# One GpSimd operation of 1024 columns fills the scan inputs of a block pair, with new engine orders and banks

## The reference

```python
xz = xn @ in_proj_w                      # 512 inner channels, then the gate z
x_c = silu(conv4(x_ssm) + conv_b)
x_dbc = x_c @ x_proj_w                   # dt (16), B (16 states), C (16 states)
dt = softplus(x_dbc[..., :R] @ dt_w + dt_b)
def step(h, inp):                        # over the 512 tokens
    xt, dtt, Bt, Ct = inp
    h = exp(dtt[..., None] * A) * h + (xt * dtt)[..., None] * Bt[:, None, :]
    return h, einsum('bn,bdn->bd', Ct, h)
y = (y + x_c * D_param) * silu(z)
x = x + alpha * attn_out + (1 - alpha) * (y @ ssm_out_w)
```

## Time and profile before

| | |
|---|---|
| median of three runs | 6051.18 us (6045.14 to 6052.57) |
| the profiled execution's own time | 6049.22 us |
| its span in the trace | 6047.2 us |
| busy share PE, DVE, POOL, ACT | 88%, 85%, 72%, 68% |
| granted TensorE clock, mean over the span | 0.959 |

### The profile page before, as it was taken

One profiled execution on the slowest core, in us unless ns is written; L12 is line 12 of the kernel. 1 busy time (PEld: TensorE's weight loads), 2 busy tenths in 40 slices (PEclk: granted clock), 3 DMA queues, 4 the chain that ended last, 5 costly groups with the idle time before them and its releaser, 6 DMA issues.

```text
span 6047.2 us, 117094 instructions
## 1 busy us (share of the span) xinstructions
PE 5294.5 (88%) x32280; PEld 3519.6 (58%) x32280; DVE 5128.6 (85%) x7776; ACT 4113.5 (68%) x6407; POOL 4329.0 (72%) x3569
## 2 busy tenths in 40 slices
...
GB/s 130 122 142 140 139 141 145 128 131 142 133 149 143 127 135 137 140 150 135 131 136 138 142 150 130 129 139 137 149 143 122 142 131 140 146 140 135 136 126 38
DMA packets 521729, 814.77 MB, mean 135 GB/s; under 512 B 80432, under 2 KB 227288, under 8 KB 520976
## 3 DMA queue, kind: packets, MB, share of 16 engines
...
q10 hardware_dynamic: 7904, 0.39, 0.1%
...
## 4 chain that ended last, share of the span: by engine, by line
PE 58%; DVE 15%; issue 11%; ACT 8%; POOL 4%; DMA 2%; ACTq 1%; SPq 1%; DVEq 0%; POOLq 0%
PE pY L939 8%; PE pM L1090 8%; PE pM L1081 6%; DVE mx L1258 4%; DVE pD L1200 4%; PE pM L1070 4%; PE pM L1014 3%; PE pM L948 3%; PE pM L961 3%; PE pM L981 3%; PE pM L1027 3%; PE pM L996 3%; PE pM L1045 2%; DMA region<-mrow 2%; ACT pD L707 2%
## 5 line engine op out<-in xcount | busy, mean ns | idle before, releaser
L584 POOL TENSOR_TENSOR state<-scan_in,bc 128x512 f32<-128x512 f32 x2048 | 2555.1, 1273 | 586.1 <-DMA bc<-bc_d 311.2
L1200 DVE TENSOR_TENSOR_SCAN pD<-pD,state 128x512 f32<-128x512 f32 x1536 | 1857.8, 1219 | 137.3 <-POOL state L584 81.0
L707 ACT ACTIVATE pD<-scan_in,A 128x512 f32<-128x512 f32 x2048 | 1403.7, 690 | 546.3 <-DVE state L1208 453.3
L939 PE MATMUL pY<-ident,state 128*128 128x128 f32 x8192 | 1209.3, 284 | 9.7 <-DVE state L1208 5.3
L939 PEld LDWEIGHTS pY<-ident,state 128*128 128x128 f32 x8192 | 944.1, 147 | 305.5 <-issue 187.4
L1208 DVE TENSOR_TENSOR state<-pD,bc 128x512 f32<-128x512 f32 x1536 | 1033.6, 682 | 27.3
L1258 DVE TENSOR_REDUCE mx<-pM 128x1 f32<-128x512 f32 (+3 forms) x1408 | 855.4, 630 | 87.1 <-PE pM L1029 81.0
L571 POOL TENSOR_TENSOR state<-state,bc 128x512 f32<-128x512 f32 x512 | 645.5, 1272 | 357.9 <-DVE state L1200 301.3
L808 ACT ACTIVATE region<-pM 128x512 f32<-128x512 f32 (+1 forms) x1408 | 742.8, 556 | 188.2 <-PE pM L1047 178.1
L1045 PE MATMUL pM<-region 98*128 98x512 bf16 (+3 forms) x2048 | 545.2, 316 | 334.4 <-DMA region<-mrow 158.7
L1200 DVE TENSOR_TENSOR_SCAN state<-pD,state 128x512 f32<-128x512 f32 x512 | 611.6, 1213 | 53.0 <-ACT pD L707 43.9
...
## 6 DMA issues: line engine op xcount, KB each, us to landing
bc<-bc_d SPq DMA_DIRECT2D x2048, 256.0 KB, 3.6
...
region<-qk_d SPq DMA_DIRECT2D x256, 64.0 KB, 2.6
...
```

Source lines behind the costliest of these rows:

```text
L584: nc.gpsimd.tensor_tensor(state[:, e % RING], us[:, parity(b), k // N * JP + e % JP, :], bc[:, k % BC_SLOTS, 0, :], ALU.mult).then_inc(b_o ...
L707: act.activation(pD[DECAY_BANK[e]][:], dts[:, parity(b), j], ACT.Exp, scale=A[:, j, n:n + 1]).then_inc(a_ok.sem, 1)
L939: ins = pe.matmul(y_part(t, e % JP), state[:, e % RING, t * P:(t + 1) * P], ident[:], is_transpose=True, start=False, stop=(e % PASS >= PA ...
L1200: v.tensor_tensor_scan(h if e in POOL_C else decay, decay, h, 0.0, ALU.mult, ALU.add)\
```

## The change

`fill_state(b, e)` becomes `fill_states(b, k)`: one operation on 1024 columns writes both ring slots of unit k, with the row of B read twice through a broadcast. It waits once for the row and once for PE, now for the later of the two slots (`e + JP - RING` is one more than before for the first slot), and its one signal raises `b_ok` by two. The lists for all five engines and the table of banks are new.

```diff
-            def fill_state(b, e):
-
-                k = e // JP
-                if e == 0:
+            def fill_states(b, k):
+
+                e, at_ = k * JP, k * JP % RING
+                if k == 0:
                     b.wait(pool, u_ok)
                 b.wait(pool, *row_in(b, k, 0))
                 if e >= RING:
-                    b.wait(pool, y_ok, e - RING + 1)
+                    b.wait(pool, y_ok, e + JP - RING)
                 else:
-                    b.wait_last(pool, y_ok, SCANS + e - RING + 1)
-                nc.gpsimd.tensor_tensor(state[:, e % RING], us[:, parity(b), k // N * JP + e % JP, :],
-                                        bc[:, k % BC_SLOTS, 0, :], ALU.mult).then_inc(b_ok.sem, 1)
+                    b.wait_last(pool, y_ok, SCANS + e + JP - RING)
+                nc.gpsimd.tensor_tensor(state[:, at_:at_ + JP], us[:, parity(b), k // N * JP:(k // N + 1) * JP, :],
+                                        bc[:, k % BC_SLOTS, 0, :].unsqueeze(1).broadcast_to([P, JP, L]),
+                                        ALU.mult).then_inc(b_ok.sem, JP)
```

Parts of the lists that are spoken of below (`fillK` is the unit K after the change):

```diff
 POOL
-  fill27 -x2 -x2b -l3s +ql0 fill28 fill29 -xb +ql1 fill30 +ql2 fill31 ... fill63 +u0 +u1 +fill0 +fill1 pc62 pc63
+  fill13 -x2 -x2b -l3s +ql0 fill14 -xb +ql1 fill15 +ql2 fill16 ... fill31 +u0 +u1 +fill0 pc62 pc63
 DVE
-  mx1_2 mx1_3 scan28 +qk1 scan29 c28 c29 +qk2 -route
+  mx1_2 mx1_3 +qk1 scan28 c28 scan29 c29 +qk2 -route
-  scan62 scan63 +scan0 +scan1 +c0 on3 +c1 gate1
+  scan62 scan63 on3 +scan0 +scan1 +c0 gate1 +c1
-  mx2_10 c43 mt2 scan44 c44
+  mx2_10 scan44 mt2 scan45 c44
-  scan58 +mx0_0 scan59 c58 on2 c59 +sp3
+  on2 scan58 +mx0_0 scan59 +mx0_1 c58 c59 +sp3
 PE
-  mx1_10 pv0_3 mt1 add29 add30 add31 mx2_0 st1_0_0
+  mx1_10 add28 mt1 add29 add30 mx2_0 pv0_2 pv0_3 add31 st1_0_0
-  mx2_10 mt2 st2_0_0
+  mx2_10 mt2 add44 st2_0_0
-  st3_1_0 +mx0_0 on2 add56 st3_1_1 add57 st3_1_2
+  st3_1_0 on2 add54 add55 st3_1_1 add56 +mx0_0 +mx0_1 add57 st3_1_2
-  add63 ot0 ot1 yt0 yt1 +skip0 +add0 +add1 yt2 yt3 +z0 +add2
+  ot0 add61 add62 ot1 add63 +z0 yt0 +skip0 +add0 yt1 yt2 +add1 yt3 +add2
 ACT (beginning of the list, where the loop's branch falls)
-  ud v0 dec2 v1 dec3 -ot0 -yt0 -ot1 -yt1 dec4 -yt2 -yt3 dec5
+  z0 dec5 dec6 ... +dec0 +v0 +dec1 +ud ot0 +dec2 ot1 +dec3 yt0 +v1 +dec4 yt1 yt2 yt3
```

More of the change, by code:

```diff
@@ L1363 @@
     "SP": """
[L1364 to L1367, removed]
+        -rb22 -rb25 -rb23 -ld3 -rc23 -rb24 -mt2 -rc25 -rb26 -rc24 -rb27 -x1p -rc26 -rc28 -rb28 -rb29 -rc27 xp
@@ L1381 @@
[L1381 to L1385, removed]
@@ new lines @@
+        dec25 +l1a zsilu dec26 dec27 st0_0_0 +xt0 +xt1 st0_0_1 dec28 st0_0_2 +qk0 dec29 st0_0_3 st0_1_0 st0_1_1
+        +qm0 -l3a st0_1_2 +qk1 -h3t0 -h3t1 +qm1 +qk2 dec30 dec31 +xs0 +qm2 +xs1 st0_1_3 +qk3 st0_2_0 +qm3 -route2
+        dec32 st0_2_2 st0_3_0 -axt dec33 -out0 dec34 -out1 dec35 mt1 dec36 dec37 st1_0_0 st1_0_1 st1_0_2 oe0
+        st1_0_3 st1_1_0 dec38 st1_1_1 dec39 st1_1_2 dec40 st1_1_3 dec41 st1_2_0 st1_2_2 dec42 st1_3_0 dec43 +xs2
+        oe1 dec44 dec45 +xs3 mt2 dec46 dec47 st2_0_0 +xsilu dec48 dec49 st2_0_1 +xp st2_0_2 st2_0_3 dec50 st2_1_0
@@ L1394 @@
[L1394 to L1403, removed]
@@ L1404 @@
-        h2t1 +add11 +add12 +add13 f1_0 f1_1 f1_2 +mx0_4 +mx0_5 f1_3 f1_4 +mx0_6 f1_5 +add14 f1_6 f1_7 +mx0_7
-        +mx0_8 +add15 +add16 +mx0_9 +add17 +mx0_10 +add18 +z3 +add19 +mt0
+        z3 mt0 add19 -f2_0 +xt0 -f2_1 mx1_0 add20 +xt1 st0_0_0 mx1_1 add21 add22 st0_0_1 st0_0_2 +qk0 st0_0_3
+        add23 st0_1_0 add24 add25 st0_1_1 mx1_2 mx1_3 +qk1 st0_1_2 -h3t0 -h3t1 +qk2 -route st0_1_3 +xs0 +xs1 +qk3
+        st0_2_0 pv0_0 pv0_1 st0_2_2 -lora add26 st0_3_0 add27 -axt mx1_4 mx1_5 -out0 mx1_6 -out1 mx1_7 mx1_8
@@ new lines @@
+        st2_1_3 pv2_0 mt3 st2_2_0 st2_2_2 pv2_1 st2_3_0 add50 pv2_2 pv2_3 st3_0_0 st3_0_1 st3_0_2 add51 add52
+        add53 st3_0_3 st3_1_0 on2 add54 add55 st3_1_1 add56 +mx0_0 +mx0_1 add57 st3_1_2 st3_1_3 pv3_0 add58 add59
+        st3_2_0 st3_2_2 st3_3_0 pv3_1 pv3_2 pv3_3 +v0 on3 +v1 add60 ot0 add61 add62 ot1 add63 +z0 yt0 +skip0
+        +add0 yt1 yt2 +add1 yt3 +add2 +add3 sso0 sso1 +add4 +add5 +z1 +add6 +mx0_2 +add7 +add8 +add9 +mx0_3
+        +add10 +add11 +z2 h2t0 h2t1 +add12 +add13 f1_0 f1_1 f1_2 f1_3 f1_4 +mx0_4 f1_5 f1_6 f1_7 +add14 +mx0_5
@@ L1406 @@
+        +mx0_6 +mx0_7 +add15 +mx0_8 +add16 +mx0_9 +add17 +mx0_10 +add18
     """,
     "DVE": """
[L1408 to L1416, removed]
@@ L1417 @@
-        +scan8 +scan9 +c8 sso0 +c9 +mx0_1 +scan10 +c10 +scan11 sso1 l2s +c11 +scan12 +c12 +mx0_2 +scan13 +c13
-        +mx0_3 +scan14 +scan15 +scan16 +scan17
+        c16 c17 +l0s scan18 c18 scan19 mx0_4 c19 scan20 c20 scan21 c21 mx0_5 mx0_6 mx0_7 mx0_8 mx0_9 mx0_10
+        scan22 +l1s scan23 scan24 mt0 scan25 c24 c25 -f2_0 scan26 -f2_1 c26 mx1_0 mx1_1 scan27 c27 -l3s +qk0
+        mx1_2 mx1_3 +qk1 scan28 c28 scan29 c29 +qk2 -route +xs0 scan30 +qk3 +xs1 -lora scan31 scan32 mx1_4 mx1_5
+        c32 scan33 mx1_6 c33 scan34 mx1_7 mx1_8 mx1_9 mx1_10 c34 mt1 scan35 mx2_0 c35 gate0 scan36 scan37 c36 c37
@@ new lines @@
+        mx2_1 scan38 scan39 scan40 scan41 c40 mx2_2 c41 scan42 mx2_3 c42 +xs2 mx2_4 scan43 mx2_5 c43 mx2_6 on0
+        mx2_7 mx2_8 mx2_9 mx2_10 scan44 mt2 scan45 c44 c45 +xs3 on1 mx3_0 scan46 mx3_1 scan47 mx3_2 mx3_3 scan48
+        scan49 c48 c49 mx3_4 scan50 mx3_5 c50 mx3_6 mx3_7 scan51 mx3_8 c51 scan52 mx3_9 c52 mx3_10 scan53 mt3 c53
+        scan54 scan55 scan56 c56 scan57 c57 on2 scan58 +mx0_0 scan59 +mx0_1 c58 c59 +sp3 scan60 c60 scan61 c61
+        scan62 scan63 on3 +scan0 +scan1 +c0 gate1 +c1 +scan2 +c2 +scan3 +c3 +scan4 +c4 +scan5 +c5 +scan6 +scan7
```

60 lines of the change are left out of this document (32 added, 28 removed).

## The result

The changed kernel takes 5940.98 us (5938.57 to 5946.19, four runs) beside 6051.88 for the kernel before: a ratio of 0.982, interval 0.9803 to 0.9837. That is 111 us or 1.8% faster, where 0.5% was forecast.

What follows compares the result with a forecast made beforehand. PE (88% busy) and DVE (85%) were taken to bound the kernel, not POOL. (-32 - 39) x 0.69 = -49, plus 10 and 7, gave -32 us: 6019 us, -0.5%; range for 8 times in 10: 5940 to 6115.

Steps and rivals of the forecast that it cites:

- The merged fill, +10 us at `fill28`: At `fill28`, where POOL has no lead, the later fill delays DVE 0.3 us a sequence: +10 us, bounds 0 and +34.
- three more such places in each sequence: Worst bound for fills elsewhere, priced at 0: three more places without lead like `fill28`, +3 x 35 = +105 us.
- `mt1`, -32, counted as -22: `pv0_2` and `pv0_3` move behind `mt1` into PE's 1.50 us round trip: -1.0 us a sequence, -32 us; bounds -1.5 and 0.
- `yt0`, -39, counted as -27: Before `yt0` on PE, `z0` in front, `v1` in bank 1 and earlier `gate1` save 1.2 us a sequence, -39 us.
- `mt2`: `add44` moves into PE's 3.11 us wait, but the maxima row comes 0.5 us later: 0, bounds 16 us either way.
- the banks of `+mx0_0` and `on2`: Of PE's bank waits of 1.40 and 1.50 us one goes, one comes with shared bank 2: 0, bounds 48 either way.
- PE's instructions are the same, so only waiting can change: Premise for pricing the new orders: only PE's waiting changes; its busy time was to stay the same within 10 us.
- the fourth rival: DVE's waits for fills go too (half of 86.7 us) and the orders give full bounds: 5900 to 5985, chance 0.15.
- the third rival: ACT's branch or shared bank 2 costs in full: +38, 6089 us, chance 0.10; sign: DVE's waits for decays grow.
- PE's and DVE's stay at the same place of the sequence, so their 4.5 us stay: The loop branches of PE and DVE, 4.5 of the 5.8 us between long and short periods, were to cost the same.
- the +7 us: ACT's branch moves from before `ud` to before `z0 dec5`, delaying `scan5`: 0.5 us for some 14 turns; bounds 0 and +29.
- The rule on the shared ports: If DVE's two-input `keep` can't run beside a POOL fill, it is 0.9 us late: +29 us, 6048, chance 0.04.

## Why the prediction was wrong

**The direction was right, and so was it that the lists and not the merged fill would bring the gain; the size was not.** The sum gave -32 us, measured are -111. The merged fill was priced at nothing for its own sake and is worth 5 us at most.

**The merged fill, +10 us at `fill28`.** In the new lists the place costs nothing. Timeline of POOL and DVE there:

```profile
2151.16 2.36 POOL L584 TENSOR_TENSOR state<-scan_in,bc 128x1024 f32<-128x1024 f32 x1
```

```profile
2153.18 0.75 DVE L1232 SCALAR_TENSOR_TENSOR dbc<-pM,qkv_b,ht 128x512 f32<-128x512 f32 x1 [2.51 <-ACT ht L751]
2153.85 1.22 DVE L1201 TENSOR_TENSOR_SCAN pD<-pD,state 128x512 f32<-128x512 f32 x1
```

The fill ends at 2153.52, `qk1` waits for ACT until 2153.18 and ends behind the fill, and the scan follows at once. So the merged fill makes nobody wait here: `qk1`, not the fill, is what the scan stands behind. Elsewhere, where the prediction had set 0, DVE does wait for a merged fill, at one place in the sequences without a branch. Timeline of DVE:

```profile
2132.81 1.23 DVE L1201 TENSOR_TENSOR_SCAN pD<-pD,state 128x512 f32<-128x512 f32 x1 [3.10 <-POOL state L584]
```

17 of the 22 waits for fills are this one, with 3.0 to 3.1 us. With split fills it is 0.96, and that run is no faster, so the 2 us between the two don't show in the time. The bound of the same term was wrong by more, for the old lists at least: +105 us at worst, and 185 to 264 measured. The bound "three more such places in each sequence" does not hold there: 68 waits in 2048 fills say how many fills were late, not by how little the others were in time.

**`mt1`, -32, counted as -22:** 14 measured. **`yt0`, -39, counted as -27:** 32 measured. Both steps held in their direction. Counting only the share of the chain that lies on PE gives 49 for the two and the runs 46; that the sum fits so well is luck, as one is 8 below and the other 5 above. The run for `yt0` moved `z0` alone; the other bank of `v1` and the earlier `gate1` were not tried by themselves.

**`mt2` and the banks of `+mx0_0` and `on2`, each priced at 0.** This is the step that failed. Taken back, the moves cost 36 and 29 us; the first is outside its bound of 16 either way. Together they are 65 of the 79 us between -32 and -111. At `mt2` the prediction set the later row of maxima against `add44` and made nothing of it. The runs show that `add44` fits into the round trip: in front of the row PE does it while the row is under way, behind the row it stands 3.19 us first. At `+mx0_0` it said that one wait goes and one comes. The runs show that `+mx0_1` is work for PE at a time when it stands for ACT behind `sp2`, and that without it the longer wait there, 2.10 us for 1.31, is followed by a stretch at the lower level of the clock. That points at a premise that failed with this step: "PE's instructions are the same, so only waiting can change". PE's busy time fell by 32 us of the 111. Moves one at a time don't add up exactly; with 5 + 14 + 32 + 29 + 36 they give 116 us of the 151 that the lists and the merged fill are worth with PE's branch hidden. The other 35 were not located.

**The range and the rivals.** 5941 us lies in the range of the fourth rival (5900 to 5985, chance 0.15), 1 us inside the lower end of the range for 8 times in 10. The fourth rival's mechanism is not what the runs show, though: it needed DVE's waits for fills halved, and they fell by 21 us; and it counted `mt1` and `yt0` in full, 71 us, where the runs show 46. Nearest is its 48 for the banks, where they show 29. That the number falls in its range is in part luck. Of the signs named, the waits before `st1_0_0` and `yt0`, the fills' 2.36 us and the sum of DVE's waits for fills came as said. DVE's 2 us before `scan28` became 2.51 us before `qk1`, for ACT. POOL's and PE's busy time did not come as said, and DVE's waits for decays grew, the sign of the third rival, while the time fell.

**The branches.** "PE's and DVE's stay at the same place of the sequence, so their 4.5 us stay" failed for PE. What a branch costs depends on what stands in front of it: `z3 add19 mt0` before, `mx0_10 add18` after. It took 40 us of the 151 back. That this is the whole reason is not shown, as with `z3 mt0 add19` in front again PE still stood 4.61 us, not 2.95. For ACT the +7 us did not show: moving its branch back before `ud` made no difference clear of noise, as its 2.25 us at `z1` only replaced 2.18 at `yt0`; that the branch before `ud` had been part of the 1.75 us at `yt0` was right.

**The rule on the shared ports** was a variant with 0.04. The mechanism shows in the trace after, where the fill beside `keep` is longer. POOL and DVE there, and DVE in the run with split fills, where POOL's two fills ended at 2160.05 + 2.49 = 2162.54:

```profile
2156.90 2.37 POOL L584 TENSOR_TENSOR state<-scan_in,bc 128x1024 f32<-128x1024 f32 x1
```

```profile
2158.87 0.45 DVE L1319 TENSOR_TENSOR keep<-lg,top 128x32 f32<-128x32 f32 x1
```

```profile
2161.87 0.72 DVE L1319 TENSOR_TENSOR keep<-lg,top 128x32 f32<-128x32 f32 x1
```

`keep` took 0.19 us before. In the changed kernel it ends at 2159.32, 0.05 us behind the fill's end of 2159.27, and in the run with split fills at 2162.59, 0.05 behind 2162.54. Median of all 32: 449 and 726 ns, and 193 before. The Trainium skill (SBUF — State Buffer, section SBUF: two separate sides) says that of a DVE operation with two SBUF inputs and a GpSimd operation that reads SBUF the one that starts first gets the shared pair of ports for the whole instruction. The trace agrees. The price was wrong: 0.26 us a sequence, 8 us in all at most, as `keep` starts late in the fill.
